# Score stage of a graph layer: a third pair of score banks, five seeded chunks, two of five pieces rounded on GpSimd, a tenth light row block

## The chip, the cores and the metric

The kernel runs on one core of one Trainium2 chip. The metric is the time of one execution on the device in microseconds, the median of several runs. The engines are TensorE (PE in the profile; PEld is its weight load), VectorE (DVE), ScalarE (ACT), GpSimd (POOL) and SyncE (SP), which here only issues DMAs.

## The reference, cut to what matters

```
def lap_mul(A, x): d = 1 / sqrt(sum(A, -1)); return d[:, None] * (A @ (d[:, None] * x))
z  = leaky_relu(lap_mul(A, x) @ W1 + b1, 0.1)                # A 8192x8192, x and z 8192x128
d2 = max(sum(z*z)[:, None] + sum(z*z)[None, :] - 2 z @ z.T, 0)
S  = exp(-sqrt(d2 + 1e-10) / 2), kept where it is among the 4 largest of its row, else 0
out = layernorm(x + lap_mul(S + A, x) @ W2 + b2)
```

Everything is float32. The S matrix has four entries a row, so the kernel never builds it: it finds the four places and gathers those rows.

## The kernel before, in words

A is stored in HBM as 16 x 16 quads of 512 x 512 elements (1 MB each, 4 contraction tiles of 128 by 512 output rows). Rows are counted in 64 tiles of 128 or 16 blocks of 512 (B), and the score stage works in 8 groups (G) of 8 tiles (GT).

Stages one and two make row sums, the first product A @ (d x) and z. They are not touched. The **score stage** then does for each of 64 tiles: TensorE multiplies the tile of z with all 8192 columns in eight chunks of 1024 (two PSUM banks, called a pair). Float32 precision is had by splitting each operand into a high half in the type fp32r and the rest, so each bank gets three matmuls (`scores`, L658 to L660) and a fourth with the squares (L662). If a chunk is *seeded*, ScalarE has written the squares into the pair beforehand (`seed`, L889), the first matmul accumulates on them, and the fourth is left out. Before, chunks 0, 2, 4 and 6 are seeded (`is_seeded`), even chunks use banks 0 and 1, odd ones banks 2 and 3, and the seed for the next even chunk is written right after an even chunk is copied out. ScalarE copies each chunk to one of two score buffers in SBUF (L904); VectorE then runs MAX8 (`find`, L1210) and FIND_INDEX8 (L1216) over all 8192 scores. Because there are two score buffers, ScalarE may copy chunk 0 of tile j only when tile j-2 has been searched (the semaphore `placed`). At a group's start VectorE has small chains besides (`chain_a`, `near_sums`, `chain_b`), which make the four weights and the scaled x of the group that has just ended and split it (xgh, xgl).

Woven into the same stage is part of the second product, A @ (d2 x), for the first HB row blocks, called **light**; the others are **heavy**. For each group and light block four *pieces* of A (128 x 1024, 512 KB) are loaded by SyncE into a ring of RAW buffers (`group_loads`, L502). ScalarE rounds a piece to its high half `ah` (`round_piece`, L872; two buffers, SPLIT), GpSimd subtracts to get the rest `al` (`rest_of_piece`, L1019), and TensorE multiplies: `piece` first does the second half of the previous piece (two matmuls with `al`, L700, waiting for `rest`), then four matmuls with `ah` (L691, L692, waiting for `rounded`). Four pieces are a unit in one PSUM bank; ScalarE flushes it (L878) and GpSimd issues a DMA that adds it to acc_dram (L1013).

The order is fixed by a table, `turn[j][c]`: in a group, cell (j, c) is chunk c of tile j, and names the pieces whose work follows that chunk. Pieces of the last two light blocks (LATE) run in tiles 0 and 1 of the group after the next, the others (4 x 7 = 28 before) in the 46 cells from (2, 2) on, piece k at cell 18 + ((k+1)*46-1)//28. In the last group all 36 are spread over those 46 cells. Every engine's queue follows the same cells. ScalarE does per cell: copy, seed if any, and for each piece of the cell the rounding of the **next** piece, then the flush. GpSimd does per piece of the cell the rest of the next piece, then the DMA issue. TensorE does the scores of the cell, then the piece.

The **tail** finishes A @ (d2 x): 14 quads of the first heavy block, the light blocks against the last group's x (two quads each, in plain float32, `plain`), then the remaining heavy blocks with 16 quads each (`plan_tail`). A halved quad (not plain) takes one rounding on ScalarE, four subtractions on VectorE and 12 matmuls. Beside this run 16 finishing jobs, one per row block, in the order FIN and at the quads FIN_AT: 16 gathers by GpSimd (L1065; two sets of buffers, freed by VectorE two jobs earlier), weighing on ScalarE (L954) seven to four quads before FIN_AT, products with W2, layer norm and store.

## Time and profile before

| | us |
|---|---|
| median of 3 runs | 2842.82 (2842.59 to 2847.33) |
| the profiled execution, its own time | 2841.84 |
| its span, first to last instruction | 2839.6 |
| stages before the first MAX8 of the score stage | 1090.6 |
| first to last MAX8 of the score stage | 1250.7 |
| last MAX8 to the end | 498.3 |
| mean granted TensorE clock | 0.968 |

Over the whole span TensorE is busy 89%, VectorE 85%, ScalarE 56% and GpSimd 35%. Such shares average over stages with different limits; a stage is read from its own windows and from which wait ends last there. A matmul's record lasts longer than its share of the engine because matmuls overlap (0.39 us of record at a pitch of 0.23), so TensorE's rate is read from the distance of starts. In a timeline, what stands in brackets is the idle time of the engine before the instruction and who ended it.

### The profile page before, as it was taken

What the parts mean: (1) busy time and instruction counts of PE and PEld (TensorE: products, weight loads), DVE (VectorE), ACT (ScalarE), POOL (GpSimd) and SP (SyncE); (2) the same over time, 40 slices, a digit from 0 to 9 for tenths busy, and PEclk for the clock granted to TensorE, in tenths of its full rate; (3) what the DMA queues carried; (4) which work ended last, traced back from release to release, by engine and by line L of the source; (5) the groups of instructions that cost most, each with busy time, mean ns of one, the idle gap of its engine ahead of it and who ended that gap; (6) DMA issues with size and microseconds to landing.
All of it is one profiled execution on the core that took longest, in us unless ns stands there. A gap on an engine that the chain in (4) does not pass through costs nothing.

```text
span 2839.6 us, 28446 instructions
## 1 busy us (share of the span) xinstructions
PE 2537.8 (89%) x9604; PEld 1778.6 (63%) x9604; DVE 2412.3 (85%) x1670; ACT 1587.8 (56%) x1809; POOL 982.9 (35%) x708
## 2 busy tenths in 40 slices
PE   0467999999899998889999999999999997998898
PEld 0133444444577776568778787878778785466665
DVE  6998899886788887999998989998999977288887
ACT  0000000001467767679989898988989884266764
POOL 0000000000000000016566565656656674667770
PEclk9778999999999999999999999999999998999999
DMA  9999999995788850014455554554454569999996
GB/s 387 422 417 381 387 421 421 421 381 202 301 322 334 333 222 30 0 60 141 132 157 142 151 149 144 148 156 135 131 161 142 172 178 407 379 364 328 355 353 227
DMA packets 142904, 716.55 MB, mean 252 GB/s; under 512 B 18433, under 2 KB 26369, under 8 KB 80321
## 3 DMA queue, kind: packets, MB, share of 16 engines
q1 hardware_dynamic: 121344, 672.85, 63.3%
q0 software_dynamic: 16832, 33.84, 5.0%
q10 hardware_dynamic: 4608, 8.39, 0.8%
q8 instruction: 61, 1.00, 0.1%
q14 instruction: 59, 0.48, 0.1%
HBM read 682.76 MB, written 32.24 MB: 252 GB/s over the span
## 4 chain that ended last, share of the span: by engine, by line
PE 59%; DVE 16%; DMA 9%; ACT 7%; issue 5%; POOL 2%; SPq 1%; ACTq 0%; DVEq 0%
PE PS L568 16%; PE PS L658 6%; PE PS L660 5%; PE PS L659 5%; DVE R L1210 5%; DVE R L1216 4%; DMA cache<-at 3%; PE PS L746 3%; PE PS L700 3%; PE PS L691 3%; PE PS L692 3%; DMA R<-at 3%; PE PS L628 3%; PE PS L662 3%; POOL R L1065 2%
## 5 line engine op out<-in xcount | busy, mean ns | idle before, releaser
L1019 POOL TENSOR_TENSOR al<-ring,ah 128x1024 fp32r<-128x1024 f32 x252 | 606.8, 2414 | 430.1 <-ACT ah L872 430.0
L1210 DVE MAX8 R<-R 128x8 f32<-128x8192 f32 x64 | 556.1, 8690 | 90.6 <-ACT R L904 88.6
L904 ACT ACTIVATE R<-PS 128x1024 f32<-128x1024 f32 x512 | 522.9, 1022 | 183.1 <-PE PS L660 106.4
L1216 DVE FIND_INDEX8 R<-R,R 128x8 uint32<-128x8192 f32 x64 | 555.8, 8685 | 0.0
L658 PE MATMUL PS<-zh,zst 128*128 128x512 f32 x1024 | 413.3, 404 | 64.6 <-ACT PS L889 57.3
L1004 POOL CAST zst<-zh 128x128 fp32r<-128x128 f32 (+1 forms) x64 | 27.5, 430 | 1219.8 <-DVE zl L1162 883.7
L659 PE MATMUL PS<-zl,zst 128*128 128x512 f32 x1024 | 403.5, 394 | 0.0
L660 PE MATMUL PS<-zh,zst 128*128 128x512 f32 x1024 | 403.3, 394 | 0.0
L568 PE MATMUL PS<-cache,R 128*128 128x512 f32 x624 | 288.4, 617 | 25.8 <-DVE R L1108 21.2
L1065 POOL DMA_INDIRECT R<-xs_dram,R x256 | 270.9, 1058 | 116.3 <-issue 81.4
L658 PEld LDWEIGHTS PS<-zh,zst 128*128 128x128 f32 x1024 | 194.8, 190 | 133.8 <-ACT PS L889 71.8
L1091 DVE TENSOR_TENSOR R<-R,cache 128x2048 f32<-128x2048 f32 x114 | 261.2, 2292 | 13.4 <-DMA cache<-at 10.8
L872 ACT ACTIVATE ah<-ring 128x1024 fp32r<-128x1024 f32 x252 | 263.8, 1047 | 9.6 <-DMA ring<-at 9.6
L889 ACT ACTIVATE PS<-R 128x1024 f32<-128x1024 f32 x252 | 259.4, 1029 | 8.0
L809 ACT ACTIVATE tiny<-rowsum 128x4 f32<-128x4 f32 x16 | 3.3, 205 | 464.7 <-DVE rowsum L1101 464.7
L568 PEld LDWEIGHTS PS<-cache,R 128*128 128x128 f32 x624 | 122.6, 198 | 179.0 <-issue 173.1
L660 PEld LDWEIGHTS PS<-zh,zst 128*128 128x128 f32 x1024 | 194.8, 190 | 42.0
L659 PEld LDWEIGHTS PS<-zl,zst 128*128 128x128 f32 x1024 | 195.4, 191 | 39.3 <-issue 1.0
L568 PE MATMUL PS<-ring,R 128*128 128x512 f32 x408 | 186.7, 606 | 19.5 <-DMA ring<-at 11.9
L662 PE MATMUL PS<-sqn,sel 128*128 128x512 f32 x520 | 203.1, 391 | 0.0
L691 PE MATMUL PS<-ah,xgh 128*128 128x512 f32 x504 | 199.0, 395 | 1.6 <-ACT ah L872 1.6
L692 PE MATMUL PS<-ah,xgl 128*128 128x512 f32 x504 | 198.5, 394 | 0.0
(146 smaller groups left out, 4183.1 us busy)
## 6 DMA issues: line engine op xcount, KB each, us to landing
ring<-at SPq DMA_DIRECT2D x157, 1024.0 KB, 8.8
R<-at SPq DMA_DIRECT2D x141, 1024.0 KB, 8.1
ring<-at SPq DMA_DIRECT2D x252, 512.0 KB, 3.8
cache<-at SPq DMA_DIRECT2D x125, 1024.0 KB, 16.4
raw_sq<-at SPq DMA_DIRECT2D x22, 1024.0 KB, 7.9
raw_z<-at SPq DMA_DIRECT2D x21, 1024.0 KB
raw_ring<-at SPq DMA_DIRECT2D x21, 1024.0 KB
acc_dram<-R POOLq DMA_DIRECT2D x63, 256.0 KB, 5.8
```

What stands on the lines that cost most here:

```text
L568: i = pe.matmul(PS[:, b % YB], xs[:, q * TB + k], slots_a[slot_of[n]][:, k], start=first and k == 0, stop=prod_at[b, q] == closed[b] and k ...
L658: pe.matmul(bank, zst[:, par, 0], zh[:, cols], start=not on_seed, stop=False, skip_group_check=True)
L659: pe.matmul(bank, zst[:, par, 0], zl[:, cols], start=False, stop=False, skip_group_check=True)
L660: i = pe.matmul(bank, zst[:, par, 1], zh[:, cols], start=False, stop=on_seed, skip_group_check=True)
L662: i = pe.matmul(bank, sel[:, cc % SQH], sqn[:, cc // SQH], start=False, stop=True, skip_group_check=True)
L691: pe.matmul(bank, xgh[:, t], ah[:, s, kk], start=p == 0 and kk == 0, stop=False)
L692: pe.matmul(bank, xgl[:, t], ah[:, s, kk], start=False, stop=False)
L904: act.activation(score[j % 2][:, c * EC:(c + 1) * EC], PS[:, 2 * (c % 2):2 * (c % 2) + 2].rearrange("p b c -> p (b c)"), ACT.Copy).then_in ...
L1019: pool.tensor_tensor(al[:, k % SPLIT], raw[k % RAW], ah[:, k % SPLIT].bitcast(F32), ALU.subtract)\
L1065: pool.indirect_dma_start(gx[f % 2][:, j, m], None, xs_dram, bass.IndirectOffsetOnAxis(ap=sidx[:, FIN[f] * TB + j, m:m + 1], axis=0))\
L1210: v.max(top[:, j], score[j % 2]).then_inc(dve3, 1)
L1216: v.max_index(place[:, j], top[:, j], score[j % 2]).then_inc(placed, 1)
```

## The change

- HB goes from 9 to 10: ten light row blocks, 40 pieces a group, 32 of them early; FIN and FIN_AT are set anew for the 116 quads that the tail then has (130 before).
- The score chunks rotate over three pairs of banks: 0 and 1, 2 and 3, 6 and 7. The units of the second product rotate over banks 4 and 5 (BANKS) instead of 4, 5 and 6.
- Chunks 3 to 7 are seeded; the seed of chunk c+3 follows the copy of chunk c. Chunks 0, 1 and 2 carry the fourth matmul.
- The ring has five raw buffers. The rest of a piece is written over the raw piece itself (`al` lies on the ring and has five buffers), so a buffer is loaded again when the product is done (`prodb`), not when the rest is.
- Of five pieces, those with k mod 5 equal to 1 or 3 are rounded by GpSimd right before it subtracts them, with the wait for two pieces earlier (`prodb`) that ScalarE had; ScalarE rounds the other three.

```
-HB = 9
+HB = 10
-FIN_AT = (27, 33, 39, 46, 52, 58, 65, 71, 77, 84, 90, 96, 103, 109, 116, 129)
+FIN_AT = (27, 33, 38, 43, 49, 54, 60, 66, 71, 77, 83, 88, 94, 100, 105, 115)
-RAW, SPLIT = 3, 2
+RAW, SPLIT, BANKS = 5, 2, 2
+SEEDED = (3, 4, 5, 6, 7)
+ON_POOL = (1, 3)
...
-        al = sb("al", [P, SPLIT, PT, BC], F32R, at=over + SPLIT * PIECE * 4)
+        al = sb("al", [P, RAW, PT, BC], F32R, at=top_of["ring"])
...
+        def wait_rounded(eng, g, k):
+            if k % RAW in ON_POOL:
+                eng.wait_ge(rounded_pool, rounds(NP) * g + rounds(k) + 1)
+            else:
+                eng.wait_ge(rounded, (NP - rounds(NP)) * g + k - rounds(k) + 1)
+        def pair(first, j, c):
+            k = c % 2 if first and j == 0 else c % 3
+            return PS[:, (0, 2, 6)[k]:(0, 2, 6)[k] + 2]
...                                                    # group_loads
-                        sp.wait_ge(rest, g * NP + (k - RAW + 1))
+                        sp.wait_ge(prodb, g * NP + (k - RAW + 1))
...                                                    # scores
-                    pe.wait_ge(seeded, NE // 2 * (GT * g + j) + c // 2 + 1 - NE // 2)
-                elif not (first and j == 0 and c < 2):
-                    pe.wait_ge(copied, NE * (GT * g + j) + c - 1)
+                    pe.wait_ge(seeded, len(SEEDED) * (GT * g + j - 1) + SEEDED.index(c) + 1)
+                elif not (first and j == 0):
+                    pe.wait_ge(copied, NE * (GT * g + j) + (-1, 0, -2)[c])
...                                                    # piece
-                pe.wait_ge(rounded, NP * g + k + 1)
+                wait_rounded(pe, g, k)
...                                                    # group_act, after the copy of chunk c
-                            seed((c // 2 + 1) % (NE // 2))
+                        if c + 3 in SEEDED and not (first and j == 0):
+                            act.wait_ge(copied, NE * (GT * g + j) + c + 1)
+                            seed(c + 3)
...
-                            if has_next(g, back, k):
+                            if has_next(g, back, k) and (k + 1) % RAW not in ON_POOL:
                                 round_piece(g - back, k + 1)
...                                                    # rest_of_piece on GpSimd
+                if k % RAW in ON_POOL:
+                    pool.wait_ge(ld_b[k % RAW], 16 * ((NP // RAW) * q + k // RAW + 1))
+                    hold(pool)
+                    if not (isinstance(g, int) and n < SPLIT):
+                        pool.wait_ge(prodb, n - SPLIT + 1)
+                        hold(pool)
+                    pool.tensor_copy(ah[:, k % SPLIT], raw[k % RAW]).then_inc(rounded_pool, 1)
+                wait_rounded(pool, q, k)
```

## Rows read from the trace of the kernel before

**Rows 1.** Windows: us, busy of PE, PEld, DVE, ACT, POOL, PEclk, DMA share, GB/s.

```profile
1711.46:1871.77 160.31, 154.98 (x666) 126.13 (x665) 147.03 (x40) 138.24 (x147) 98.33 (x61) 0.98 0.51 146
1090.63:2341.30 1250.67, 1185.08 (x5044) 952.38 (x5044) 1148.19 (x301) 1056.06 (x1109) 687.55 (x436) 0.98 0.44 130
2341.30:2839.60 498.30, 435.86 (x1691) 299.48 (x1690) 368.48 (x747) 269.44 (x383) 291.70 (x263) 0.97 0.92 344
```

**Rows 2.** Timeline of VectorE in the fifth group: start, duration, engine, line, operation.

```profile
1731.54 3.43 DVE L1260 TENSOR_TENSOR R<-R,tiny 128x1024 f32<-128x1024 f32 x1
...
1754.66 8.67 DVE L1210 MAX8 R<-R 128x8 f32<-128x8192 f32 x1
...
1852.81 8.70 DVE L1210 MAX8 R<-R 128x8 f32<-128x8192 f32 x1 [1.89 <-ACT R L904]
```

**Rows 3.** Timeline of TensorE and ScalarE around tile 3 of that group.

```profile
1752.00 0.39 PE L662 MATMUL PS<-sqn,sel 128*128 128x512 f32 x1
1757.01 0.80 PE L658 MATMUL PS<-zh,zst 128*128 128x512 f32 x1 [4.62 <-ACT PS L889]
...
1766.21 0.39 PE L660 MATMUL PS<-zh,zst 128*128 128x512 f32 x1
1766.44 0.39 PE L658 MATMUL PS<-zh,zst 128*128 128x512 f32 x1
...
1754.87 1.02 ACT L904 ACTIVATE R<-PS 128x1024 f32<-128x1024 f32 x1 [4.81 <-DVE R L1216]
1755.92 1.03 ACT L889 ACTIVATE PS<-R 128x1024 f32<-128x1024 f32 x1
```

**Rows 4.** Windows after the stall in the second and in the fifth group.

```profile
1276.00:1280.00 4.00, 1.17 (x6) 0.66 (x5) 4.00 (x2) 2.75 (x3) 0.00 (x0) 1.00 0.30 111
1280.00:1284.00 4.00, 4.00 (x19) 3.31 (x18) 4.00 (x1) 3.97 (x5) 2.41 (x1) 1.00 0.06 8
...
1757.00:1763.00 6.00, 6.00 (x14) 4.72 (x15) 6.00 (x1) 4.83 (x6) 2.38 (x1) 0.51 0.21 59
1763.00:1775.00 12.00, 12.00 (x54) 9.94 (x53) 9.09 (x3) 9.55 (x12) 7.99 (x4) 1.00 0.49 126
```

**Rows 5.** Groups of instructions: busy us, mean ns; or ns min/median/max.

```profile
L872 ACT ACTIVATE ah<-ring 128x1024 fp32r<-128x1024 f32 x252 | 263.8, 1047 | 9.6 <-DMA ring<-at 9.6
...
L878 ACT ACTIVATE R<-PS 128x512 f32<-128x512 f32 x63 | 36.8, 584 | 3.5 <-DMA acc_dram<-R 3.5
L1013 POOL DMA_DIRECT2D acc_dram<-R x54 | 46.1, 853 | 3.7 <-ACT R L878 3.7
L1301 DVE TENSOR_TENSOR R<-R 128x1024 f32<-128x1024 f32 x16 | 19.6, 1227 | 2.1 <-ACT R L954 1.9
...
L1004 POOL CAST zst<-zh x64: 279/293/2202, 884.2 to 2301.5; 128x128 fp32r<-128x128 f32 x32, 128x128 fp32r x32
...
L1019 POOL TENSOR_TENSOR al<-ring,ah x252: 2375/2404/3472, 1216.1 to 2339.5; 128x1024 fp32r<-128x1024 f32 x126
```

**Rows 6.** Timeline of TensorE: first and last quad of the last six row blocks.

```profile
2481.15 0.47 PE L755 MATMUL PS<-ah_t,xsh 128*128 128x512 f32 x1
...
2826.30 3.60 PE L746 MATMUL PS<-raw_sq,R 128*128 128x512 f32 x8
```

**Rows 7.** Gathers: the group, then the first and the last of 256.

```profile
L1065 POOL DMA_INDIRECT R<-xs_dram,R x256 | 270.9, 1058 | 116.3 <-issue 81.4 <-DVE R L1304 26.7 <-DMA xs_dram<-R 8.2
...
2394.77 1.41 POOL L1065 DMA_INDIRECT R<-xs_dram,R  x1 [8.16 <-DMA xs_dram<-R]
...
2770.71 0.94 POOL L1065 DMA_INDIRECT R<-xs_dram,R  x1 [0.30 <-issue]
2771.96 1.79 POOL L1065 DMA_INDIRECT R<-xs_dram,R  x1 [0.30 <-issue]
```

**Rows 8.** DMA queue, 2400 to 2800 (packets, MB, share); then a wait from 2500 on.

```profile
q1 hardware_dynamic: 16274, 118.44, 76.9%
...
ACT R L954 <- DMA R<-xs_dram,R: 17.4, 4, 7.1
```

More of the change, by code:

```diff
@@ L404, in is_seeded, with rounds @@
         def is_seeded(first, j, c):
-            return c % 2 == 0 and not (first and j == 0)
+            return c in SEEDED and not (first and j == 0)
+        def rounds(k):
+            return sum(i % RAW in ON_POOL for i in range(k))
+        def wait_rounded(eng, g, k):
[6 more added lines that the diff above has]
+            return PS[:, (0, 2, 6)[k]:(0, 2, 6)[k] + 2]
         def is_first(n):
@@ L649, in scores @@
                 on_seed = is_seeded(first, j, c)
+                if first and j == 1 and c == 0:
+                    pe.wait_ge(sq_row_ok, len(SEEDED))
                 if on_seed:
-                    pe.wait_ge(seeded, NE // 2 * (GT * g + j) + c // 2 + 1 - NE // 2)
-                elif not (first and j == 0 and c < 2):
-                    pe.wait_ge(copied, NE * (GT * g + j) + c - 1)
+                    pe.wait_ge(seeded, len(SEEDED) * (GT * g + j - 1) + SEEDED.index(c) + 1)
+                elif not (first and j == 0):
+                    pe.wait_ge(copied, NE * (GT * g + j) + (-1, 0, -2)[c])
+                elif c >= 2:
+                    pe.wait_ge(copied, c - 1)
                 for h in range(2):
                     cc = 2 * c + h
-                    bank = PS[:, 2 * (c % 2) + h]
+                    bank = pair(first, j, c)[:, h]
                     cols = slice(cc * BC, (cc + 1) * BC)
@@ L666, in squares_row @@
             def squares_row(i):
+                c = SEEDED[i]
                 if i < 2:
                     pe.wait_ge(copied, NE - 1 + i)
-                else:
-                    pe.wait_ge(sq_row_ok, i - 1)
+                elif i >= 3:
+                    pe.wait_ge(sq_row_ok, i - 2)
                 for h in range(2):
-                    cc = 4 * i + h
-                    m = pe.matmul(PS[:, 2 * (i % 2) + h], sel[:, cc % SQH], sqn[:, cc // SQH], start=True, stop=True)
+                    cc = 2 * c + h
+                    m = pe.matmul(pair(False, 0, c)[:, h], sel[:, cc % SQH], sqn[:, cc // SQH], start=True, stop=True)
                 m.then_inc(sq_rows, 1)
@@ L717, in group_pe @@
                         if is_first(g) and (j, c) == (0, NE - 1):
-                            for i in range(NE // 2):
+                            for i in range(len(SEEDED)):
                                 squares_row(i)
@@ L877, in flush_unit @@
                     act.wait_ge(s_acc, 16 * (HB * g + ib))
[L878 removed]
+                act.activation(flush, PS[:, 4 + ib % BANKS], ACT.Copy).then_inc(flushed, 1)
             def copy_squares(i):
@@ L882, in copy_squares, with seed @@
                 act.wait_ge(sq_rows, i + 1)
[L883 to L890 removed]
+                act.activation(sq_row[SEEDED[i]], pair(False, 0, SEEDED[i]), ACT.Copy).then_inc(sq_row_ok, 1)
+            def seed(c):
+                act.activation(pair(False, 0, c), sq_row[c], ACT.Copy).then_inc(seeded, 1)
             def group_act(g):
@@ L903, in group_act @@
                         act.wait_ge(gram, NE * (GT * g + j) + c + 1)
-                        act.activation(score[j % 2][:, c * EC:(c + 1) * EC],
-                                       PS[:, 2 * (c % 2):2 * (c % 2) + 2].rearrange("p b c -> p (b c)"),
-                                       ACT.Copy).then_inc(copied, 1)
+                        act.activation(score[j % 2][:, c * EC:(c + 1) * EC].rearrange("p (b c) -> p b c", b=2),
+                                       pair(first, j, c), ACT.Copy).then_inc(copied, 1)
                         if first and (j, c) == (0, NE - 1):
-                            for i in range(NE // 2):
+                            for i in range(len(SEEDED)):
                                 copy_squares(i)
-                            act.wait_ge(sq_row_ok, NE // 2)
-                            seed(0)
-                        if c % 2 == 0 and not (first and j == 0) and (c < NE - 2 or not (is_last(g) and j == GT - 1)):
+                            act.wait_ge(sq_row_ok, len(SEEDED))
+                        if c + 3 in SEEDED and not (first and j == 0):
                             act.wait_ge(copied, NE * (GT * g + j) + c + 1)
-                            seed((c // 2 + 1) % (NE // 2))
+                            seed(c + 3)
                         if first and (j, c) == (0, 0):
```

31 lines of the change are left out of this document (12 added, 19 removed).

## The prediction

> **What bounds the kernel now.** I read the windows of the stages first, then VectorE's timeline, and only where that shows an idle stretch TensorE's and ScalarE's. The score stage takes 1250.67 us and the tail 498.30 us of the span [rows 1]; the change touches only these two. One steady group of the score stage takes 160.31 us, with both TensorE (154.98 us) and VectorE (147.03 us) nearly full [rows 1]. Call P the start of tile 2's MAX8 (1754.66), which is the end of tile 1's search [rows 2]. From the MAX8 of the last tile, 7, of the group before (1852.81 less the group's 160.31) to P the searches and small chains follow each other with hardly a gap: 62.2 us that VectorE sets. From P to the next tile 7's MAX8 (1852.81) are 98.1 us in which TensorE sets the pace: VectorE waits for scores before every search.
>
> TensorE's pitch there is 0.23 us a matmul: 1766.21 to 1766.44, and 54 in 12.00 us when it never stops [rows 3, 4]; I use 0.2265. Around P it stands still: its last matmul before starts at 1752.00, the next at 1757.01 [rows 3]. The reason is a chain in ScalarE's queue. Chunk 0 of tile 3 may be copied only once tile 1 is searched, because there are two score buffers; so ScalarE waits 4.81 us, then copies, then seeds, and only then chunk 2 may start. After these 4.6 idle us the granted clock is 0.51 (the 1.2 GHz level) for the next 6 us, in which 14 matmuls go instead of 26; an idle stretch of 2.8 us in the group before two others was followed by 1.00 [rows 4]. So the one stall costs 4.6 us and some 3 more.
>
> Check of this account: after P, TensorE has 42 score matmuls of tile 3, four pieces (24), 224 of tiles 4 to 7 and 19 pieces (114) before the last copy, 404 in all, 91.5 us; with 2.3 of ScalarE's chain, 3.2 for the clock and 1.1 for the last copy it gives 98.1.
>
> **The change, score stage.** Seeding five of eight chunks makes a tile 54 matmuls instead of 56. A tenth light row block makes 40 pieces a group instead of 36, each six matmuls. Together 672 instead of 664, +1.8 us a group. Where they fall matters more.
>
> With three pairs of banks, chunks 0, 1 and 2 need no seed and run ahead of P. But the piece table then blocks in another place. With 32 early pieces they fall at chunks (2,3), (2,4), (2,6), (2,7), (3,1), (3,2), (3,4), (3,5), (3,6) and on. Piece 5 at (3,2) needs its high half, 5 mod 5 is 0, so ScalarE rounds it, and in ScalarE's order this stands in cell (3,1): behind copy 0, seed 3, copy 1 and seed 4, all of which wait for P. Copy and seed take 1.02 and 1.03 [rows 3], a rounding 1.05 [rows 5], and the first copy started 0.2 after P: P + 5.3 us. TensorE gets there with 12 matmuls more than before (16 more of tiles 2 and 3, 4 fewer of 0 and 1; 2.7 us later than 1752.4 is P + 0.4), so it idles 4.9 us, about as long as before, and I expect the same low clock after it. Third pair and all, the stall stays.
>
> After P + 5.3 there are 4 matmuls of piece 5, 30 of chunks 3 to 7, three pieces (18), 216 of tiles 4 to 7 and 22 pieces (132): 400, four fewer than before (-0.9). The chain is 5.3 where it was 2.3 (+3.0). Sum +2.1 us a group.
>
> The second term is what ScalarE and GpSimd deliver. ScalarE per tile: 8 copies, 5 seeds, 0.6 of 5.6 roundings and 1.4 flushes (0.58) [rows 3, 5] are 17.7 us of TensorE's 19.8; hidden in sum, but in chunks 0 to 4 copy and seed of every cell stand ahead of its rounding. Followed through tile 4, piece 12's rounding ends 0.8 us after TensorE wants it, elsewhere 0.2 at most; I take 0.35 a tile over four tiles, 1.4 a group. GpSimd's rounding is an operation the trace does not have. Nearest rows: its cast of 128 columns has a median of 293 ns, its subtraction of 1024 columns 2404 [rows 5]. From below, 0.3: eight times the columns can't be cheaper than the cast. From above 2.4, the subtraction. I take 1.1: the cast's time grows with its columns by an unknown part, a tenth of a us for 128 if most is fixed, and the cast row is the nearer, since it is the same operation. Then GpSimd has, per five pieces, 12.0 of subtractions, 2.2 of casts, 1.1 of accumulating DMA issues (853 ns) and 0.5 of stationary casts, 15.8 us where TensorE takes about 17.5. It fits, with casts waiting behind the previous subtraction but rarely late.
>
> The Trainium skill (GPSIMD Engine Reference, Performance versus the Vector engine) puts a tight loop at about 1.8 cycles an element; an estimate from it is 1.5 us for this cast, and the trace of before neither confirms nor denies it. By that GpSimd would stand at 16.6 us of 17.5, the casts would be late more often, and the sum would be some 7 us more. The same page (When to use GPSIMD) calls one-input work roughly line-rate, an estimate of 1.0 and a sum as below.
>
> The loads: a raw slot is freed by the product instead of the subtraction, but there are five slots, so a load is issued three pieces (10 us) ahead of its rounding; the 9.6 us that roundings waited for loads in all [rows 5] may go, and lay before P, where they cost nothing. SyncE's stores of the split x move behind two more loads; they are read only in the tail. No seed crosses a tile end any more. These cost nothing.
>
> Five steady groups at +3.5 are +17.5. The second group idled only 2.8 us without losing the clock [rows 4]; it gets the longer chain and perhaps the low clock, +3. The first has no pieces and is VectorE's: 0, the fifth squares copy standing against a seed that goes. In the last group 40 pieces fall in 46 cells; piece 6 at (3,2) is GpSimd's there, so it does not wait for P, the stall shrinks under 1 us and the clock should hold (-6), while GpSimd with 3.1 us a piece over some 34 pieces is as long as TensorE and late here and there (+6): 0. Score stage: **+21 us**.
>
> **The change, tail.** A tenth light block turns 14 quads with halved matrices away (84 to 70 after the first 14), and leaves 32 plain ones. The 96 quads of the last six row blocks ran from 2481.15 to 2829.7, 3.63 us each [rows 6]; 80 at that pace, behind two more plain quads in the light part (3.5 each), save 16 x 3.63 - 7 = 51 us. Against this stands the queue of gathers. They go from 2394.77 to 2771.96 [rows 7], 256 at a pitch of 1.25 us where nothing disturbs them (0.94 of it the issue); with the mean of 1058 ns instead [rows 7] the 240 up to the fifteenth block (index 14) are 300 + 27, and half of the 26.7 us of waits for buffers [rows 7] adds 13: they end at 2735, landed by 2740, as seen from the same start. Quads at 3.63 would reach that block's weighing (quad 98) at 2487 + 62 x 3.63 = 2712. So ScalarE waits there or before, 28 us in all, and the last 17 quads can win back little: at 3.4 each, between 12 matmuls (2.7) and 3.63, they end 58 us later, and 9.9 us after it the kernel: 2808, a gain of 31. DMA bounds it likewise: 118.44 MB of the big queue are 76.9% of 400 us [rows 8], 2.6 us per MB, so 14 MB are 36 us, and the DMA share of the tail is 0.92 [rows 1]. I take **-36 us**; ends -20 (gathers slower) and -52.
>
> Sum: +21 - 36 = -15. The profiled execution took 2841.84 us (2839.6 of span and 2.2 around it), so 2827; it stood 1 us below the median, so **2828 us**.
>
> **Rivals.**
> (a) The banks do what three pairs suggest: TensorE reaches P without a long idle stretch, the clock holds. For it: the 1.00 after 2.8 idle us [rows 4]. Against it: piece 5's place behind ScalarE's wait. Then 3 and 3.2 us a group go and small lateness too: about -3 a group, six groups -18, with the tail's -36 in all -54: 2788. Chance 0.15.
> (b) The tail is not held by gathers, with its waits hidden by the extra quads at the end: -51, so 2813. For it: ScalarE waited for gathers only 17.4 us after 2500 before [rows 8]. Chance 0.15.
> (c) Slower: GpSimd becomes the bound of tiles 3 to 7. It decides from a cast of about 1.9 us, where five pieces cost it 17.4 us. At 2.4 they cost 18.4, 3.7 a piece; 27 pieces after P + 5 are 104 us against TensorE's 101.6, with lateness on both sides +8 a group, and the last group +14: score stage +62, total +26: 2869. For it: the subtraction's 2404 ns, and that operations of both engines stretch when they meet: VectorE's 128x1024 multiply took 3.43 beside GpSimd's, and an addition of that shape 1.23 elsewhere [rows 2, 5]. Against: the 293 ns. Chance 0.2.
> (d) The change does not do what it says in the tail: gathers keep the pace of before, waits included (23.6 us a block), and the tail gains only some 20: +1, 2844. Chance 0.07.
> The forecast itself has 0.43, its own range 2812 to 2846.
>
> **How the numbers follow.** No change is anything within 0.2% (5.7 us), which a measurement of this kernel can just tell. Faster: 0.31 of the forecast's 0.43, all of (a), 0.14 of (b), sum 0.60. Slower: (c), 0.02 of (d), 0.05 of the forecast, sum 0.27. Same: the other 0.13. The range 2793 to 2864 leaves out a part of (a) and of (c).
>
> **What would show it.** Right: TensorE idle 4 to 5 us near P with piece 5's matmul (line of the high half) waiting for ScalarE's rounding, low clock after it; groups of 163 to 165 us; GpSimd's cast at 1.0 to 1.3 us; tail some 36 us shorter with ScalarE's weighing waiting for gathers. Wrong: groups under 158 us (a); matmuls of both halves waiting for GpSimd many times a tile (c); GpSimd's gathers with gaps and the tail at 446 us (b). A clock that holds after piece 5's wait would take 3 us off each group.

## The result, and the profile after

The changed kernel takes 2900.55 us (median of 4, 2900.24 to 2905.94) where the kernel before, beside it, takes 2844.46: a ratio of 1.0205, 95% interval 1.0193 to 1.0218. It is slower by 2%. Forecast were 2828 us, range 2793 to 2864: wrong in sign, and outside the range.

First come the windows of a steady group, of the score stage (first to last MAX8) and of the tail, the same columns as [rows 1], which they answer:

```profile
1724.04:1894.78 170.74, 160.28 (x673) 126.92 (x672) 152.69 (x41) 134.99 (x144) 123.94 (x83) 0.98 0.52 151
1092.37:2421.56 1329.19, 1229.90 (x5088) 958.25 (x5088) 1182.89 (x302) 1037.87 (x1096) 865.29 (x583) 0.98 0.46 135
2421.56:2898.70 477.14, 402.21 (x1524) 272.10 (x1522) 335.71 (x693) 242.39 (x368) 280.25 (x263) 0.95 0.89 328
```

The score stage grew by 78.5 us (forecast +21), the tail shrank by 21.2 (forecast -36). To see where, I read the starts of the MAX8 in VectorE's timeline and take their distances in a steady group, the fifth. Column P is the sum of the first three (tile 7 to tile 2, the forecast's "62.2 us that VectorE sets"), column Q that of the other five (of the rounded distances, so 0.1 us can be lost):

| kernel | 7-0 | 0-1 | 1-2 | 2-3 | 3-4 | 4-5 | 5-6 | 6-7 | P | Q |
|---|---|---|---|---|---|---|---|---|---|---|
| before | 19.0 | 25.7 | 17.5 | 20.4 | 19.5 | 19.5 | 19.3 | 19.5 | 62.2 | 98.2 |
| after | 23.0 | 27.3 | 17.5 | 21.3 | 20.0 | 21.3 | 19.3 | 21.0 | 67.8 | 102.9 |

Over the stage, P grew by 34.6 us in six groups. Q grew by 27.2 in the five steady ones, by 8.0 in the second, and by 10.2 in the last, where tiles take 24 us instead of 21. The first group, where no piece falls, is 1.5 us shorter. The second group has no late pieces at its start, so GpSimd subtracts nothing beside VectorE's chains there, and all their small instructions take 0.17 to 0.19 us: its P is 60.2 us in both kernels, and in every kernel below (60.3 at most). So the 62.2 us of the kernel before already held 2 us that come with GpSimd's work.

Why P grew is in VectorE's timeline of the stretch from tile 7 to tile 2 (start, duration, line, operation):

```profile
1723.98 8.69 DVE L1236 MAX8 R<-R 128x8 f32<-128x8192 f32 x1 [3.35 <-ACT R L925]
...
1741.62 1.51 DVE L1248 TENSOR_SCALAR R<-R 128x32 f32<-128x32 f32 x1
1743.29 0.83 DVE L1249 TENSOR_TENSOR R<-R,sq 128x32 f32<-128x32 f32 x1 [0.16 <-DVE R L1248]
1744.15 0.18 DVE L1251 TENSOR_SCALAR R<-R 128x32 f32<-128x32 f32 x1
1744.38 2.26 DVE L1253 COPY R<-R 128x32 uint32 x1
1746.98 8.70 DVE L1236 MAX8 R<-R 128x8 f32<-128x8192 f32 x1 [0.35 <-DVE R L1253]
...
1755.82 0.19 DVE L1267 TENSOR_REDUCE tiny<-R 128x8 f32<-128x32 f32 x1
1756.13 1.82 DVE L1268 TENSOR_TENSOR tiny<-tiny,rowsum 128x8 f32<-128x8 f32 x1
...
1767.93 2.27 DVE L387 TENSOR_SCALAR tiny<-tiny 128x8 f32<-128x8 f32 x1
```

And this is GpSimd's of the same stretch:

```profile
1740.69 2.39 POOL L1045 TENSOR_TENSOR al<-ring,ah 128x1024 fp32r<-128x1024 f32 x1 [1.46 <-ACT ah L896]
...
1743.04 1.03 POOL L1043 CAST ah<-ring 128x1024 fp32r<-128x1024 f32 x1
1744.15 2.45 POOL L1045 TENSOR_TENSOR al<-ring,ah 128x1024 fp32r<-128x1024 f32 x1
...
1755.53 2.40 POOL L1045 TENSOR_TENSOR al<-ring,ah 128x1024 fp32r<-128x1024 f32 x1
...
1767.76 2.41 POOL L1045 TENSOR_TENSOR al<-ring,ah 128x1024 fp32r<-128x1024 f32 x1
```

The same places in the kernel before, VectorE first, then GpSimd:

```profile
1710.14 0.18 DVE L1222 TENSOR_SCALAR R<-R 128x32 f32<-128x32 f32 x1
...
1710.94 0.18 DVE L1227 COPY R<-R 128x32 uint32 x1
...
1720.61 0.17 DVE L1242 TENSOR_TENSOR tiny<-tiny,rowsum 128x8 f32<-128x8 f32 x1
```
```profile
1707.17 2.41 POOL L1019 TENSOR_TENSOR al<-ring,ah 128x1024 fp32r<-128x1024 f32 x1 [1.88 <-ACT ah L872]
1711.71 2.41 POOL L1019 TENSOR_TENSOR al<-ring,ah 128x1024 fp32r<-128x1024 f32 x1 [2.12 <-ACT ah L872]
...
1731.48 2.40 POOL L1019 TENSOR_TENSOR al<-ring,ah 128x1024 fp32r<-128x1024 f32 x1 [1.46 <-ACT ah L872]
```

Instructions on 32 or 8 columns, 0.17 to 0.19 us elsewhere, take up to 2.3 us, and each long one ends when a GpSimd subtraction ends: 1741.62 + 1.51 = 1743.13 against 1743.08, 1744.38 + 2.26 = 1746.64 against 1746.60, 1767.93 + 2.27 = 1770.20 against 1770.17. The one of 0.83 us ends with GpSimd's cast (1744.12 against 1744.07). Before, the first chain ran in the gap between two subtractions (1709.58 to 1711.71); the change moved it into GpSimd's working time. The 3.43 us multiply of [rows 2] started 0.06 us behind a subtraction of 2.40 us and is the same thing in the kernel before; after the change it takes 1.23, which is why the distance 0-1 grew by less than 2 us.

The Trainium skill has the rule (SBUF — State Buffer, "SBUF: two separate sides"): VectorE and GpSimd share a pair of ports, and when the VectorE instruction is in a mode that uses two ports, or has two inputs in SBUF, whichever engine starts first keeps the pair for a whole instruction and "the other fully blocks". This trace agrees on the waiting, with the ends above; it doesn't show the ports.

The stall at P has the cause that was forecast. These are TensorE's row (piece 5, the line of the high half), ScalarE's two before it, and the window after:

```profile
1792.05 1.03 ACT L925 ACTIVATE R<-PS 128x1024 f32<-128x1024 f32 x1 [4.49 <-DVE R L1242]
...
1796.08 1.04 ACT L896 ACTIVATE ah<-ring 128x1024 fp32r<-128x1024 f32 x1
```
```profile
1797.17 0.50 PE L715 MATMUL PS<-ah,xgh 128*128 128x512 f32 x1 [3.00 <-ACT ah L896]
```
```profile
1798.00:1804.00 6.00, 6.00 (x21) 4.78 (x20) 5.85 (x3) 4.73 (x6) 5.85 (x4) 0.72 0.35 44
```

P is 1791.84, and 1797.17 is P + 5.33 where P + 5.3 was forecast; TensorE idled 3.0 us instead of 4.9, and the granted clock fell for a part of the next six (0.72, with 21 matmuls where before there were 14 at 0.51). GpSimd's cast (ns, min/median/max; its mean is 1112) is what I took, 1.1:

```profile
L1043 POOL CAST ah<-ring x112: 1027/1043/1366, 1249.0 to 2416.4; 128x1024 fp32r<-128x1024 f32 x112
```

In the tail, these are the first and last gather and ScalarE's wait for them after 2540 (answering [rows 7, 8], whose wait is from 2500 on):

```profile
2472.20 1.05 POOL L1091 DMA_INDIRECT R<-xs_dram,R  x1 [7.35 <-DMA xs_dram<-R]
...
2839.40 0.94 POOL L1091 DMA_INDIRECT R<-xs_dram,R  x1 [0.30 <-issue]
```
```profile
ACT R L973 <- DMA R<-xs_dram,R: 87.5, 11, 23.6
```

The gathers take 367.2 us from first to last start, 377.2 before. ScalarE waits 87.5 us for them instead of 17.4; over the whole tail it is 113.8 instead of 66.1.

### The profile page after: what moved, and what is told of

Same layout as the page of the kernel before. It is cut to its first block, busy times and chain, and to the rows that moved or that the text cites. A ratio compares the mean times of both kernels' runs of the same rounds, so it can differ in the third digit from the quotient of the medians.

```text
span 2898.7 us, 28749 instructions
## 1 busy us (share of the span) xinstructions
PE 2549.2 (88%) x9480; PEld 1756.7 (61%) x9480; DVE 2414.2 (83%) x1616; ACT 1542.5 (53%) x1781; POOL 1149.2 (40%) x855
## 4 chain that ended last, share of the span: by engine, by line
PE 44%; DVE 18%; issue 12%; DMA 9%; POOL 8%; ACT 7%; SPq 1%; DVEq 0%; ACTq 0%; POOLq 0%
PE PS L587 15%; DVE R L1236 6%; POOL R L1091 4%; DVE R L1242 4%; DMA cache<-at 3%; PE PS L681 3%; PE PS L683 3%; PE PS L682 3%; PE PS L770 3%; DMA R<-at 3%; PE PS L647 3%; PE PS L715 3%; ACT R L925 2%; PE PS L716 2%; POOL al L1045 2%
## 5 line engine op out<-in xcount | busy, mean ns | idle before, releaser
L1045 POOL TENSOR_TENSOR al<-ring,ah 128x1024 fp32r<-128x1024 f32 x280 | 672.5, 2414 | 288.7 <-ACT ah L896 279.6
L1023 POOL CAST zst<-zh 128x128 fp32r<-128x128 f32 (+1 forms) x64 | 23.3, 365 | 1219.2 <-DVE zl L1188 885.6
L911 ACT ACTIVATE PS<-R 128x1024 f32<-128x1024 f32 x315 | 324.2, 1029 | 10.0
L587 PE MATMUL PS<-cache,R 128*128 128x512 f32 x624 | 288.9, 618 | 25.3 <-DVE R L1134 21.2
L1091 POOL DMA_INDIRECT R<-xs_dram,R x256 | 259.2, 1013 | 116.3 <-issue 82.1
L715 PE MATMUL PS<-ah,xgh 128*128 128x512 f32 x560 | 231.0, 413 | 61.4 <-ACT ah L896 39.4
L681 PEld LDWEIGHTS PS<-zh,zst 128*128 128x128 f32 x1024 | 197.5, 193 | 96.6 <-ACT PS L911 43.1
L716 PE MATMUL PS<-ah,xgl 128*128 128x512 f32 x560 | 221.8, 396 | 0.0
L1196 DVE TENSOR_TENSOR al<-ring,ah 128x2048 fp32r<-128x2048 f32 x69 | 157.9, 2291 | 43.7 <-ACT ah L868 43.1
L724 PE MATMUL PS<-al,xgh 128*128 128x512 f32 x560 | 178.8, 401 | 8.2 <-POOL al L1045 8.2
```

What stands on the lines that cost most here:

```text
L587: i = pe.matmul(PS[:, b % YB], xs[:, q * TB + k], slots_a[slot_of[n]][:, k], start=first and k == 0, stop=prod_at[b, q] == closed[b] and k ...
L681: pe.matmul(bank, zst[:, par, 0], zh[:, cols], start=not on_seed, stop=False, skip_group_check=True)
L715: pe.matmul(bank, xgh[:, t], ah[:, s, kk], start=p == 0 and kk == 0, stop=False)
L716: pe.matmul(bank, xgl[:, t], ah[:, s, kk], start=False, stop=False)
L911: act.activation(pair(False, 0, c), sq_row[c], ACT.Copy).then_inc(seeded, 1)
L1045: pool.tensor_tensor(al[:, k % RAW], raw[k % RAW], ah[:, k % SPLIT].bitcast(F32), ALU.subtract)\
```

## The experiments

The theory is that VectorE's small instructions stand behind GpSimd's, and that the change moved them there. The rival is that GpSimd's new load (casts) or the tenth block is at fault by itself, through late halves for TensorE. For the tail, the theory is that gathers set it, the rival that matmuls or matrix loads do. The edits are shown shortened.

The experiments ran on four chips. On three of them the medians of before are 2917.65 to 2935.45 us, on the fourth 2844.31. The longer time lies in the tail: on the three, kernels with nine light blocks and all gathers have tails of 573 to 592 us (498 in the profile of before), and those with ten 563 to 601 (477 in the changed kernel). The score stages don't differ: e14 and e15, which leave them as they are, have 1328.9 and 1250.6 us. So ratios below are blurred by the tail, those of kernels with ten blocks most, which lose there some or all of what the tenth block gained, and score stages are compared in the traces: "stage" is first to last MAX8, 1250.7 us before and 1329.2 after.

**The change, taken apart.** e1 is the changed kernel with all roundings on ScalarE, e2 the kernel before with only the banks and seeds (and so two banks for the light units, where a group's first unit also waits for the last flush), e7 with only the tenth block (and its raw slots), e4 the change with nine blocks, e3 the kernel before with one idle 128x1024 cast more on GpSimd for two of five pieces.

```diff
e1  -ON_POOL = (1, 3)             +ON_POOL = ()
e2  -NE // 2 seeds, 2 pairs       +SEEDED = (3, 4, 5, 6, 7), pair(...); HB = 9, RAW = 3 stay
e7  -HB = 9; RAW, SPLIT = 3, 2    +HB = 10; RAW, SPLIT, BANKS = 5, 2, 2; FIN, FIN_AT of the change
e4  -HB = 10; RAW = 5             +HB = 9; RAW = 4; FIN, FIN_AT of before; the rest of the change stays
e3  +if k % 5 in (1, 3): pool.tensor_copy(al[...], raw[...])    # in rest_of_piece, then overwritten by the rest
```

> The changed kernel with ON_POOL = (), so that ScalarE rounds every piece; all else as changed (five raw buffers, ten light blocks, three pairs of banks). Port theory: the changed kernel lost some 5.7 us a group because VectorE's small instructions at the group's start (MAX8 of tile 7 to MAX8 of tile 0, then to tile 1) stand behind GpSimd's instructions; without GpSimd's casts (1.1 us each) it is idle more often, and tile 7 to tile 0 falls from 23.0 to 19 to 21 us, tile 0 to tile 1 from 27.35 to 25 to 26. Supply theory: the loss lies in late high halves; then with ScalarE at 17.6 + 2.3 us a tile of 20 it gets worse from P to tile 7 (103.0 to 106 us or more) and both first intervals stay. Total by the port theory alone about 2880 us, by the supply theory above 2910; both may act.

> The kernel before with three pairs of score banks and chunks 3 to 7 seeded, nothing else: nine light blocks, three raw buffers, ScalarE rounds all (with nine units on two banks the first unit of a group also waits for the last flush). Idle near P should be about 3 us, since the piece at (3,2) waits for a rounding behind copy 0 and seed 3 only, the clock may hold, and 22 matmuls fewer stand after P: P to tile 7 from 98.1 to 91 to 94 us; if VectorE's chains keep their 18.9 and 25.7 us intervals, the total is 2795 to 2815. If seeding five chunks costs as such (ScalarE late), P to tile 7 stays at 98 or more and the total is at 2845 or above.

> The kernel before, with one more cast of 128x1024 on GpSimd ahead of the subtraction in two of five pieces (its result is overwritten by the subtraction; the output is the same). Port theory: GpSimd is busy more of the group's start, so some of VectorE's small instructions take 1 to 2.4 us instead of 0.18, and the two first intervals (18.9 and 25.7 us) grow by 1 to 4 us together: 2850 to 2875. Supply theory: GpSimd has 3.4 us idle in each such place, the later subtraction makes TensorE wait at the rest half now and then, the intervals stay, and P to tile 7 grows by 0 to 2 us: 2845 to 2860. Whether a cast meets VectorE's chain depends on where it falls; the trace decides, not the total.

> The change with nine light row blocks instead of ten (four raw slots; casts at pieces 1 and 3 of every five; the order of finished rows is that of before). It is the banks and seeds of before-plus-banks, plus GpSimd's casts and subtractions that overwrite the raw piece. Theory (each part adds its own): score stage as banks-and-seeds alone (last search at 2370.0) plus some 10 us for the casts beside VectorE's chain, so 2375 to 2390; ratio to before 1.010 to 1.016; steady groups 165 to 167 us. Rival (the casts relieve ScalarE, 91% busy in the banks-only kernel, and only the tenth block made GpSimd too full): last search at 2350 to 2368, ratio under 1.008.

> The kernel before with the tenth light block alone: ten light blocks, five raw slots that the rests overwrite, the new order of finished rows, two banks for light products; score banks, seeds and ScalarE's roundings as before. Theory (the tenth block costs more in the score stage than its 24 matmuls a group at 0.2265 us, 5.4 us, and gives 21 us in the tail): steady groups 164 to 166 us, last group some 8 us longer, last search 25 to 35 us later than before (2366 to 2376), ratio 1.001 to 1.005. Rival (the tenth block is cheap without the new banks, as the pieces fall into TensorE's idle time before P): steady groups at most 162 us, last search at 2345 to 2356, ratio 0.993 to 0.998.

| kernel | stage | P | Q | last group's Q | ratio to before |
|---|---|---|---|---|---|
| e2 banks, seeds | 1280.3 | 65.3 | 98.6 | 110.8 | 1.0085 [1.0058, 1.0112] |
| e7 tenth block | 1272.6 | 62.2 | 101.3 | 109.6 | 1.0074 [1.0051, 1.0098] |
| e1 both | 1312.0 | 64.8 | 104.1 | 114.0 | 1.0161 [1.0102, 1.022] |
| e3 casts alone | 1258.5 | 63.3 | 97.1 | 111.6 | 1.0007 [0.9985, 1.0028] |
| e4 change, 9 blocks | 1271.9 | 67.3 | 96.6 | 106.8 | 1.0094 [1.0061, 1.0126] |
| after | 1329.2 | 67.8 | 102.9 | 116.1 | 1.0205 |

The banks and seeds cost 29.6 us of the stage; the tenth block 21.9 alone and 31.7 on top of them; the casts 17.2 more; 21 was the forecast for all three together. e2's interval 2-3 did fall, from 20.4 to 18.2, but more was lost elsewhere, and its result is the rival's of its expectation. e7's last search (2365.5) is 0.5 us below its theory's range and its ratio above it. e1 fits neither theory whole: 0-1 at 25.0 is the first one's, 7-0 at 22.4 missed its 19 to 21, and P to tile 7 at 103.8 in the mean is the second one's. e3's two intervals grew by 1.1, the lower edge of its theory, while Q fell by about 1 in a steady group and grew by 5.6 in the last group. e4's last search (2366.0) lies in its rival's range, its ratio between the two: with nine blocks the casts on GpSimd save 8.4 us of the stage against e2, since Q falls by 2 and by 4 in the last group, more than P's 2 cost; with ten blocks they cost 17.2. So no one part is at fault.

Two things are seen apart. P grows with every kernel that has the new banks (e2, with no cast on GpSimd: 65.3), and not with the tenth block alone (62.2). And casts on two of five pieces lengthen P by 1.1 in the old order (e3) but by 3.0 in the new one (the changed kernel against e1), which makes 17.9 us in six groups, as much as their whole 17.2. The place of the work counts as well as its amount.

**Holding GpSimd back.** e5 makes GpSimd wait at cell (0,5) of the changed kernel until the chain behind tile 7 is done; e6 also at (1,2) for the sums of near distances and at (2,3) for the gathered x.

```diff
+for at_cell, s in (((0, 5), idx_ok), ((1, 2), r2_ok), ((2, 3), xg_ok)):    # e5: the first alone
+    if (j, c) == at_cell: pool.wait_ge(s, g); hold(pool)
```

> The changed kernel with one wait more: in every group but the first, GpSimd goes on at cell (0,5) only after VectorE's first small chain (the four instructions between tile 7's search and tile 0's). Port theory: those four take 0.96 us again instead of 5, the interval of tile 7 to tile 0 falls from 23.0 to 19 us, six or seven groups gain 3 to 4 us: 2872 to 2885. If the interval is set by late scores, it stays at 23 and GpSimd's delay of up to 2 us makes the total 2900 to 2915.

> The changed kernel, with three waits more in GpSimd's order in every group but the first: at cell (0,5) until the chain behind tile 7's search is done, at (1,2) until the next chain is, at (2,3) until the gathered x has its high halves. In these three stretches GpSimd runs no subtraction and no cast. Theory (VectorE's small instructions stand behind GpSimd's running one): the stretch from tile 7's MAX8 to tile 2's goes from 67.8 us back to 62 to 64 a group, TensorE has spare time there, and the last search of the score stage starts 20 to 30 us earlier than with the change (at 2391 to 2402 us instead of 2421.6). Rival (GpSimd cannot afford to stand still): it loses 2 to 5 us at each wait, halves come late, tiles 3 to 7 take up what was gained, and the last search starts at 2415 to 2430.

In e5, 7-0 is 19.0 again, but 0-1 grew from 27.3 to 30.8, since the next small instructions now met the subtractions that had been put off: the stage is 1326.1, only 3.1 us less than the changed kernel's, where some 16 to 28 had been expected; ratio 1.0277 [1.0233, 1.0321], with a tail of 570.5 us. In e6, 7-0 is 19.0 and 0-1 27.3, P 63.8, stage 1302.5: 26.7 us back for three waits and no work taken away; ratio 1.0159 [1.0102, 1.0216]. Q stays at 102 to 103.5, so GpSimd could afford to stand still: the theory's numbers.

**The meeting made on purpose.** The kernel before, with one wait and no operation more:

```diff
+if not is_first(g) and (j, c) == (0, 5): pool.wait_ge(placed, GT * g); hold(pool)
```

> The kernel before with one wait more and no operation more: at cell (0,5) GpSimd waits until tile 7's search is done, so that the subtraction that used to end just before VectorE's chain starts with it. Theory (a small VectorE instruction waits until GpSimd's running one ends): one instruction of that chain takes 1.5 to 2.4 us instead of 0.18, and the interval from tile 7's MAX8 to tile 0's grows from 19.0 to 20.5 to 21.5 us a group in all six groups, with TensorE's work untouched; nothing else moves by over 0.3 us. Rival (chain times grew for another reason, the banks or the clock): the chain stays at 19.0 +- 0.2.

7-0 grew from 19.0 to 23.0 to 23.3 us in five of six groups (21.0 in the other), more than the expected 20.5 to 21.5 because two subtractions then ran in a row. This is VectorE's and GpSimd's timeline of it:

```profile
1717.51 0.18 DVE L1225 TENSOR_SCALAR R<-R 128x32 f32<-128x32 f32 x1
1717.85 2.43 DVE L1226 TENSOR_TENSOR R<-R,sq 128x32 f32<-128x32 f32 x1 [0.16 <-DVE R L1225]
1720.32 2.32 DVE L1228 TENSOR_SCALAR R<-R 128x32 f32<-128x32 f32 x1
1722.56 0.32 DVE L1230 COPY R<-R 128x32 uint32 x1
```
```profile
1717.82 4.78 POOL L1019 TENSOR_TENSOR al<-ring,ah 128x1024 fp32r<-128x1024 f32 x2 [5.17 <-DVE R L1219]
```

The first instruction, ahead of the subtraction, takes 0.18; the next two take one subtraction each. The stage is 1265.0, 14.3 longer; ratio 1.0025 [1.0011, 1.0039]. With the banks, the casts and the block count untouched, this shows the mechanism by itself. Not all else stood still, as had been expected: 0-1 fell to 24.2, as the multiply now met no subtraction (1.23 us instead of 3.43), and Q fell by 4.5 us in the five steady groups together.

**ScalarE's order.** e2 lost time in tiles 3 to 7 too (20.7, 20.4, 19.3, 20.0). TensorE's waits there name ScalarE's roundings (us, times, longest):

```profile
PEld PS L702 <- ACT ah L883: 5.5, 6, 1.7
PE PS L702 <- ACT ah L883: 3.2, 4, 1.3
```

e8 is e2 with the rounding ahead of the cell's seed; e9 has the three holds as well. (The copy still comes first in both; the expectation of e8 puts it too strongly.)

```diff
 act.activation(score..., pair(first, j, c), ACT.Copy).then_inc(copied, 1)
+for back, k in pieces_at(g, j, c): round_piece(g - back, k + 1)      # was behind the seed
 if c + 3 in SEEDED: seed(c + 3)
```

> The kernel with three pairs and five seeds alone (nine blocks), with ScalarE's rounding of a cell put ahead of the cell's copy and seed (the rest of the order as it was). Theory (tiles 3 to 7 lose because the rounding stands behind copy and seed): the 20.7, 20.4, 19.3, 20.0 us of tiles 3 to 7 go back to 19.3 each, 3 us a group, last search some 15 us earlier than with the banks alone (at 2353 to 2358 instead of 2370.0). Rival (ScalarE at 91% is short of time whatever its order): copies and seeds are late instead, the same intervals within 0.5 us, last search at 2366 to 2374; or later, if a rounding ahead of copy 0 delays P's chain.

> The kernel with nine light blocks, three pairs and five seeds, ScalarE's rounding ahead of the cell's seed (its copy stays first), and GpSimd's three waits: at cell (0,5) for the chain behind tile 7, at (1,2) for the sums of near distances, at (2,3) for the gathered x. Theory (what is left of the loss is VectorE's small instructions behind GpSimd's): the 21.9 and 25.5 us of the group's first two intervals become 19.0 and 23.5, the others stay at 17.8 to 19.2; first to last MAX8 1215 to 1225 us where the kernel before has 1250.7 and e8_round_first 1244.7; ratio to before 0.985 to 0.992, so faster than both kernels. Rival (TensorE needs the late halves at once): intervals of 19.0 and 27 as in e6_holds, 1230 to 1240 us, ratio 0.992 to 0.996.

e8 has tiles 3 to 7 at 19.1, 19.2, 19.0, 19.1, Q 94.3 and a stage of 1244.7, 35.6 us less than e2, more than the 15 expected; ratio 0.9984 [0.9964, 1.0004]. So ScalarE's order, and not its amount of work, held e2's tiles up. e9 has 7-0 at 19.0, but 0-1 at 27.3, the rival's intervals: the stage is 1241.3, only 3.4 us less than e8; ratio 0.996 [0.9946, 0.9974], 0.4% below the kernel before on a chip whose tail is like the first's.

**The second chain.** In e9 the subtractions of cells (1,5) and (1,7) meet the chain that scales the gathered x. e16 moves the third hold to (1,7), until x is scaled; e13 puts the late pieces a cell earlier and holds at (0,6), (1,2) and (1,6); e17 lets the last hold last until x is split.

```diff
e16 -((2, 3), xg_ok, g)                  +((1, 7), dve3, (GT + CHA + CHB) * g + 1)
e13 -at_k = (2 * k + 1) * NE // late     +at_k = 2 * k * NE // late
    +((0, 6), idx_ok, g), ((1, 2), r2_ok, g), ((1, 6), dve3, (GT + CHA + CHB) * g + 1)
e17 -((1, 6), dve3, ...)                 +((1, 6), xg_ok, g)
```

> e9_round_first_holds with the eight late pieces of a group one cell earlier (cells 0, 2, ... 14 of the first two tiles instead of 1, 3, ... 15) and the holds at (0,6) for the chain behind tile 7, (1,2) for the near sums, and (1,6), where GpSimd waits until the gathered x is scaled. Theory (the 27.3 us of tile 0 to tile 1 are 23.7 plus VectorE's instructions that stand behind the subtractions of cells (1,5) and (1,7)): that interval falls to 23.7 to 25.0, tiles 3 to 7 stay at 94.3 us; first to last MAX8 1222 to 1232 us where e9 has 1241.3; ratio to before 0.989 to 0.994. Rival (a later subtraction holds up piece 0, and with it tile 2, or another instruction is met): the interval stays over 26.5 or tile 2 to 3 grows by as much, 1238 to 1245 us.

> e9_round_first_holds with only its third hold moved: from (2,3) to (1,7), where GpSimd waits until the gathered x is scaled. Theory: the subtraction of cell (1,5) still meets the chain (1.5 us), that of (1,7) no longer does (2.2 us): tile 0 to tile 1 takes 25.0 to 25.6 us instead of 27.3, first to last MAX8 1229 to 1236 us. Rival: as e9, 1238 to 1245 us.

> e13_late_pieces_early with the hold at (1,6) lasting until the gathered x is split in halves, not only scaled. Theory: the cast of 2.89 us goes back to 0.69, tile 0 to tile 1 from 25.7 to 23.5 to 23.9 us, VectorE's part from 62.4 to 60.2 to 60.8, first to last MAX8 1216 to 1222 us where e13 has 1229.7; ratio to before 0.984 to 0.989. Rival (piece 0's low half comes 2 to 3 us later and holds TensorE up near tile 2): tile 2 to tile 3 grows by 1.5 to 2 us, 1225 to 1231 us, ratio as e13 (0.990).

e16 failed: 0-1 stayed at 27.2, since the subtraction that no longer met the chain met the cast behind it (2.88 us instead of 0.69); stage 1243.0, ratio 0.9964 [0.9939, 0.9989]. In e13, 0-1 is 25.7, above the expected 25.0, for the same reason, P is 62.4 and the stage 1229.7, in the range; ratio 0.9901 [0.9866, 0.9936], the lowest of all. What was left is one row of VectorE, and one of GpSimd:

```profile
1722.20 2.89 DVE L1283 CAST xgh<-R 128x1024 fp32r<-128x1024 f32 x1 [0.31 <-DVE R L1278]
```
```profile
1722.13 2.41 POOL L1032 TENSOR_TENSOR al<-ring,ah 128x1024 fp32r<-128x1024 f32 x1 [4.72 <-DVE R L1278]
```

In e17 the cast takes 0.69 and 0-1 is 23.5, but 1-2 grows from 17.5 to between 19.0 and 20.2, where VectorE waits for scores:

```profile
1747.07 8.70 DVE L1228 MAX8 R<-R 128x8 f32<-128x8192 f32 x1 [2.18 <-ACT R L912]
```

So the rival's time came, one interval earlier than it had said: once the chains are short, TensorE and ScalarE set P too. The stage is 1229.6, as e13's; ratio 0.9932 [0.9913, 0.9951] on another chip.

**The changed kernel, mended.** e11 is the changed kernel with e9's order and holds, e18 with e17's, e12 is e9 with the tenth block and no cast on GpSimd.

```diff
e11  after + round_piece ahead of the seed + the holds of e6
e18  e11 + at_k = 2 * k * NE // late + the holds of e17
e12  e11, -ON_POOL = (1, 3)   +ON_POOL = ()
```

> The changed kernel (ten light blocks, GpSimd rounds two of five) with the three waits of GpSimd and with ScalarE's own roundings ahead of the cell's seed. e6_holds (waits alone) has 1302.5 us from the first MAX8 to the last; tiles 3 to 7 of a steady group took 103 to 104.6 us. Theory (supply to TensorE is what is left, half of it ScalarE's order): 100 to 101.5 us for tiles 3 to 7, 1280 to 1290 us in all. Rival (it is GpSimd's own order, casts behind subtractions, that is late): 103 us and over as before, 1298 to 1305 us.

> The changed kernel (ten light blocks, GpSimd rounds two of five) with ScalarE's roundings ahead of the cell's seed, the late pieces one cell earlier and the three holds of e17. Theory (the whole loss of VectorE's part is the meeting of the engines): from tile 7's MAX8 to tile 2's 60.1 to 61 us instead of 67.8 in the changed kernel, tiles 3 to 7 as in e11 (98 to 99); first to last MAX8 1244 to 1252 us where e11 has 1269.1 and the changed kernel 1329.2. Rival (with ten blocks the late pieces can't be held so long): the part stays over 62.5 or tiles 3 to 7 take over 100.5, 1258 us or more.

> As e9_round_first_holds, but with the tenth light block of the change (five raw slots that the rests overwrite, ScalarE rounds all forty pieces). Theory (the tenth block costs 24 matmuls a group, 5.4 us at 0.2265 us, wherever TensorE sets the pace, as e7_hb10_only showed with 3.2 to 4 us a group): first to last MAX8 22 to 32 us longer than e9_round_first_holds. Rival (with the stall at tile 2 gone it costs the full 5.4 us and ScalarE, above 91% busy, adds lateness): 35 to 50 us longer.

| kernel | 7-0 | 0-1 | 1-2 | P | Q | stage | ratio to before |
|---|---|---|---|---|---|---|---|
| after | 23.0 | 27.3 | 17.5 | 67.8 | 102.9 | 1329.2 | 1.0205 |
| e11 | 19.0 | 27.2 | 17.5 | 63.7 | 98.4 | 1269.1 | 1.0002 [0.9992, 1.0011] |
| e18 | 19.8 | 23.5 | 17.5 | 60.8 | 98.0 | 1251.1 | 0.9982 [0.9959, 1.0004] |
| e12 | 19.0 | 27.5 | 17.5 | 64.0 | 99.5 | 1273.1 | 1.0019 [1.001, 1.0028] |

e18 and e12 came out as their theories said; e11 came out below its theory's 1280 to 1290 us. e18 does all the work of the changed kernel, GpSimd's casts and the tenth block included, and its stage is 78.1 us shorter by order alone. Of these, e6's holds gave 26.7, ScalarE's order 33.4 (e11 against e6), and the earlier late pieces with the longer holds 18.0 (e18 against e11). Of 78.5 us lost nothing is left in sum: Q is still 9.7 us longer than before over the stage, 5.2 of it in the last group, and P 7.9 shorter. e12 minus e9 is 31.8 us of stage for the tenth block; their tails, on one chip, are 485.5 and 497.7 us.

**The tail.** e14 and e15 leave out two of the four gathers a tile from the third row block on (144 instead of 256), after and before; ScalarE's wait counts down with them. Each was executed once, both on the same chip of the long tail.

```diff
-for m in range(KNN):      +for m in range(KNN if f < 2 else KNN // 2):
```

> The changed kernel with two of the four gathers a tile left out from the third row block of the tail on (144 gathers instead of 256); the sums are made of what is in the buffers, all other work as it was. Theory (the gathers held the tail: 259 us of issue and ScalarE's 114 us of waits for them): ScalarE's waits for gathers fall under 25 us and the tail from 477 to 440 to 455 us, which is the -51 us that the matmuls alone would have given. Rival (the matrix loads or TensorE set the tail anyway): 468 to 477 us.

> The kernel before with the same half of the gathers left out. Theory (with nine light blocks the gathers hold the tail only a little, 17.4 us of waits after 2500): the tail falls from 498.3 to 480 to 495 us, so that with half of the gathers the tenth block is worth 35 to 50 us and with all of them 21. Rival (gathers hold both tails alike): it falls by as much as in e14.

The windows of both tails, e14 first:

```profile
2423.48:2880.40 456.92, 395.21 (x1524) 267.71 (x1522) 334.60 (x693) 242.56 (x368) 166.86 (x151) 0.96 0.88 326
```
```profile
2343.41:2854.60 511.19, 437.13 (x1692) 300.63 (x1690) 367.15 (x747) 269.41 (x383) 170.33 (x151) 0.95 0.87 321
```

With tails of 456.9 and 511.2 us, the tenth block is worth 54 us when half of the gathers are gone, where the matmuls alone had been worked out at 51. With all of them it gave 21 on the first chip and 12 in e12 against e9; on the chips of the long tail it gave 13 on one (e1 and e5 against e2 and e3, means) and lost 4 to 5 on another (e6, e7, e18 against e4, e8, e17). No kernel with ten blocks and all gathers ran on the chip of e14 and e15. The sizes themselves missed: e14 is 2 us above its range, with 49.4 us of ScalarE's waits for gathers instead of under 25, and e15 is 16 above. With nine blocks too, half of the gathers took 67 us off the tail of that chip (578.2 in e16), so there gathers hold both tails, which was the rival of e15; what stands is that they leave the kernel with ten blocks less of its gain.

## Why the prediction was wrong, point by point

- **The step that failed** is "From the MAX8 of the last tile ... to P ... 62.2 us that VectorE sets", carried over as unchanged. It measured 67.9, and that is 34.6 of the 57.5 us that the score stage missed by. I had read that VectorE sets this stretch and then costed only TensorE's, ScalarE's and GpSimd's queues. What the runs showed instead: its small instructions wait for GpSimd's running one, so the stretch depends on when GpSimd works (e10 lengthened it to 65.0 by one wait, e6 cut it to 63.8 and e18 to 60.8). The multiply of 3.43 us [rows 2] was used in rival (c) as a sign of contention, but only for GpSimd's throughput, not for VectorE's chain.
- **P to tile 7, +3.5 forecast, +5.4 measured** in a steady group. The mechanism, piece 5 behind ScalarE's wait at P + 5.3, was right to 0.03 us, and e11 against e6 shows what the order of rounding and seed costs: with it changed, Q falls from 102.9 to 98.6 in the mean of five groups. The four distances from tile 3 to tile 7 grew by 3.8 us, as forecast (ten matmuls more, 2.3, and 1.4 of lateness). The size that was off is tile 2 to tile 3, where 14 matmuls fewer and a chain 3.0 longer make -0.2 and the mean of five groups is +1.6: behind P + 5.33 the 52 matmuls took 14.6 us, where 11.8 is their pace at the full clock. The lower clock is part of it, though it cost less than the 3.2 taken, and a wait of 0.25 us for GpSimd's cast is a small part; the rest is not taken apart.
- **Last group, 0 forecast, +10.2 after P and +6.1 before it.** The stall was to give 6 us, and tile 2 to tile 3 gave 0.7; lateness was to cost 6, and the four distances behind it grew by 10.9. e7 and e2 show +3.5 and +4.8 after P, e1 +8.0, so it is mostly block and banks, the casts adding 2. In the second group +3 was forecast and +8.0 measured.
- **The cast at 1.1** measured 1112 ns in the mean: right, and rival (c), which decided from 1.9, did not come. The time came out beyond it all the same, by another mechanism.
- **The tail, -36 taken, -21.2 measured.** The mechanism was right (gathers hold it: ScalarE's 113.8 us of waits, and e14 against e15). The sum worked out was -31 and I took 5 more from the big queue's bytes, which did not bind: e14 moved the same 129.8 MB of that queue in a tail of 456.9 us instead of 477.1. Of the other 10, gathers at the pace forecast (363 us for 256 against 367.2) explain 4. The rest lies behind the fifteenth block, where 64 us went from its weighing (2824.68) to the last transposes (2888.95) instead of 58; why is not shown.
- A rival of the right kind, VectorE's chain in GpSimd's way, was missing from the prediction, and with it a price for the time to come out beyond (c)'s 2869.

It stays open why the tail is longer on three of the chips. Leaving out half of the gathers took 67 us off one of them, so gathers have a part in it.

## What to carry to other kernels

When VectorE sets a stretch, list its short instructions and lay GpSimd's timeline beside them; any re-timing of GpSimd, even without more work, can put a 2.4 us wait into a 0.2 us instruction. Such a wait counts as busy time, so look at the longest duration of a short instruction against its shortest. Let GpSimd wait at the few places where such a chain runs. Fill buffers that feed the bound engine before those that only run ahead, as the rounding before the seed. In e18 three waits and two moves gave back 78 us of the changed kernel's score stage, and the move of the rounding was the largest part.

## What was not expected of the hardware

Only some of VectorE's instructions are stopped. MAX8 and FIND_INDEX8 keep 8.67 to 8.70 us beside GpSimd's subtractions in every kernel, and a reduction of 32 columns took 0.19 beside one (1755.82 in the kernel after). Copies (0.18 to 2.26), casts (0.69 to 2.89), tensor-scalar (0.17 to 2.27) and tensor-tensor forms (0.17 to 1.82 on 8 columns, 1.23 to 3.43 on 1024) wait for its end. It goes the other way too: GpSimd's cast of 128 columns, 0.29 us, took 1.32 beside VectorE's subtraction in e13. And a subtraction put off to spare one instruction met the next (e5, e16), so here holds paid only when they covered the chains behind too (e6, e18).
